# Vision tower with routed experts: when VectorE numbers the slots of the last two images

## The reference, cut to what matters

```python
probs = jax.nn.softmax(t @ Wr, axis=-1)
idx = jnp.argmax(probs, axis=-1)
onehot = jax.nn.one_hot(idx, E, dtype=jnp.int32)
pos = jnp.sum(jnp.cumsum(onehot, axis=0) * onehot, axis=-1) - 1
kept = pos < cap
flat = idx * cap + jnp.minimum(pos, cap - 1)
disp = jnp.zeros((E * cap, D), t.dtype).at[flat].add(t * kept[:, None].astype(t.dtype))
ein = disp.reshape(E, cap, D)
h = jax.nn.relu(jnp.einsum('ecd,edf->ecf', ein, W1))
eout = jnp.einsum('ecf,efd->ecd', h, W2).reshape(E * cap, D)
```

## Time and profile before

| | |
|---|---|
| time, median of 3 runs | 251.41 us (251.34 to 252.23) |
| profiled execution, its own time | 251.09 us |
| its span in the profile | 249.3 us |
| PE busy | 232.7 us (93%) |
| DVE busy | 183.8 us (74%) |
| ACT busy | 151.6 us (61%) |
| POOL busy | 98.1 us (39%) |

### The profile page before, as it was taken

How to read it: one execution, slowest core, us unless ns; L and a number is a source line. 1 busy time by engine, 2 the same in 40 slices (tenths; PEclk the granted TensorE clock), 3 DMA queues, 4 the chain that set the end, 5 groups by cost and what they waited for, 6 DMA issues and landing times.

```text
span 249.3 us, 4995 instructions
## 1 busy us (share of the span) xinstructions
PE 232.7 (93%) x1673; PEld 223.1 (89%) x1673; DVE 183.8 (74%) x557; ACT 151.6 (61%) x354; POOL 98.1 (39%) x169
## 2 busy tenths in 40 slices
PE   6999999999999999878799999999999999999940
PEld 5899999999999998647799999999999999999940
DVE  4885697887979799786456796749967678779540
ACT  5336567787877786465665477656775758656100
POOL 7000227584665658438100020156260332513662
PEclk9999999999999999999999999999999999999995
DMA  5939563174896020201499919257092460100100
GB/s 175 289 100 304 137 206 135 38 233 148 246 378 224 2 83 15 68 0 43 118 338 293 383 56 313 68 164 261 0 300 93 140 229 3 45 2 24 35 4 0
DMA packets 28378, 35.48 MB, mean 142 GB/s; under 512 B 2780, under 2 KB 25291, under 8 KB 28354
## 3 DMA queue, kind: packets, MB, share of 16 engines
q1 hardware_dynamic: 26144, 31.71, 39.9%
q0 software_dynamic: 1792, 3.47, 3.9%
q10 hardware_dynamic: 418, 0.00, 0.1%
HBM read 26.97 MB, written 9.47 MB: 146 GB/s over the span
## 4 chain that ended last, share of the span: by engine, by line
PE 75%; DMA 5%; DVE 5%; issue 5%; POOL 5%; ACT 2%; POOLq 1%; ACTq 0%; SPq 0%; DVEq 0%
PE bank L1274 14%; PE bank L1276 14%; PE bank L1275 14%; PE bank L1345 14%; PE bank L1399 4%; PE bank L1362 4%; POOL out_dram L573 3%; DMA bqc<-in_L_attn_bq_dram 2%; PE bank L1524 2%; DMA dispatched<-trow,slot 2%; PE bank L1574 2%; PE bank L1415 1%; PE bank L1373 1%; PE bank L1417 1%; PE bank L1416 1%
## 5 line engine op out<-in xcount | busy, mean ns | idle before, releaser
L1191 DVE SCALAR_TENSOR_TENSOR h_lo<-bank,h_hi 128x320 fp32r<-128x320 f32 x58 | 28.3, 488 | 27.4 <-ACT h_hi L817 24.8
L817 ACT ACTIVATE h_hi<-bank 128x320 fp32r<-128x320 f32 x58 | 25.3, 436 | 35.4 <-PE bank L1276 35.4
L573 POOL DMA_INDIRECT out_dram<-tokens_mem,images x24 | 28.0, 1168 | 37.9 <-ACT tokens_mem L834 17.1
L1274 PE MATMUL bank<-einT_hi,w_hi 128*128 128x320 f32 x128 | 40.6, 317 | 0.6 <-DVE einT_lo L1183 0.3
L1275 PE MATMUL bank<-einT_lo,w_hi 128*128 128x320 f32 x128 | 39.5, 308 | 0.0
L1276 PE MATMUL bank<-einT_hi,w_lo 128*128 128x320 f32 x128 | 39.5, 308 | 0.0
L947 DVE TENSOR_TENSOR w_lo<-w_raw,w_hi 128x1024 fp32r<-128x1024 f32 x32 | 38.8, 1214 | 0.0
L1274 PE MATMUL bank<-h_hi,w_hi 128*128 128x320 f32 x112 | 35.2, 314 | 0.1
L1276 PE MATMUL bank<-h_hi,w_lo 128*128 128x320 f32 x112 | 34.6, 309 | 0.0
L1275 PE MATMUL bank<-h_lo,w_hi 128*128 128x320 f32 x112 | 34.6, 309 | 0.0
L745 ACT ACTIVATE w_hi<-w_raw 128x1024 fp32r<-128x1024 f32 x32 | 33.7, 1052 | 0.0
(11 more groups left out here) (231 smaller groups left out, 577.3 us busy)
## 6 DMA issues: line engine op xcount, KB each, us to landing
w_raw<-in_L_ffn_W_dram SPq DMA_DIRECT2D x16, 1024.0 KB, 7.8
images<-in_x_dram SPq DMA_DIRECT2D x7, 768.0 KB, 4.8
dispatched<-blank SPq DMA_DIRECT2D x4, 645.0 KB, 8.6
images<-dispatched SPq DMA_DIRECT2D x9, 258.0 KB, 7.2
out_dram<-lone SPq DMA_DIRECT2D x8, 256.0 KB, 7.6
images<-in_x_dram SPq DMA_DIRECT2D x2, 384.0 KB, 5.1
images<-dispatched SPq DMA_DIRECT2D x9, 64.5 KB, 7.1
out_dram<-tokens_mem,images POOLq DMA_INDIRECT x24, 2.5
```

What stands on the lines that cost most here:

```text
L573: pool.indirect_dma_start(out_rows, bass.IndirectOffsetOnAxis(ap=ein[0:n, e, j, D + 1:D + 2].bitcast(U32), axis=0), z[0:n, e % 2, j, :], N ...
L817: act.activation(hidden_halves(n)[0], bank[n % 2][:, 0:CAP], ACT.Relu).then_inc(h_hi_ready, 1)
L1191: dve.scalar_tensor_tensor(lo, bank[n % 2][:, 0:CAP], 0.0, hi.bitcast(F32), ALU.max, ALU.subtract).then_inc(h_ready, 1)
L1274: pe.matmul(to, ah, bh, start=first, stop=False)
```

## The change

Four edits, all in VectorE's list:

1. In `route` the comparison with the largest gate and the product with `rank` (two instructions of 16 columns, one after the other, over tile `hit`) become one fused form for each half of the tokens (two instructions of 8 columns, with `lmax` as per-partition scalar). `lsub` moves behind `onehot`.
2. `keys_low(L)` stands ahead of `residual(L - 1)` and the two `residual_in(L, ...)`, no longer behind them.
3. `number` is cut in two: `add_places` (for images 6 and 7 `base`, and the sum `place`) and the rest. `add_places(L - 1)` stands between `softmax_sum(L)` and `late_residual()`.
4. The rest of `number(L - 1)` stands ahead of `compare(L)`, behind `factor(L - 1)`.

```diff
                 link(dve.tensor_reduce(lmax[:, :], gate[:, :, :], AX_X, ALU.max))
-                peak = lmax[:, :].unsqueeze(2).broadcast_to([P, SC, E])
-                step(dve.tensor_tensor(hit[:, :, :], gate[:, :, :], peak, ALU.is_equal))
-                if b >= 1:
-                    dve.wait_ge(lexp_ready, b)
-                dve.tensor_tensor(lsub[:, :, :], gate[:, :, :], peak, ALU.subtract).then_inc(lsub_ready, 1)
+                for s in range(SC):
+                    step(dve.scalar_tensor_tensor(hrank[:, s, :], gate[:, s, :], lmax[:, s:s + 1], rank[:, s, :],
+                                                  ALU.is_equal, ALU.mult))
                 settle()
-                link(dve.tensor_tensor(hrank[:, :, :], hit[:, :, :], rank[:, :, :], ALU.mult))
                 if b >= 2:
                     dve.wait_ge(tallied, b - 1)
                 link(dve.tensor_reduce(best[:, b % 2], hrank[:, :, :], AX_X, ALU.max))
                 dve.tensor_tensor(onehot[:, b % 2], rank[:, :, :],
                                   best[:, b % 2].unsqueeze(2).broadcast_to([P, SC, E]), ALU.is_equal
                                   ).then_inc(onehot_ready, 1)
+                if b >= 1:
+                    dve.wait_ge(lexp_ready, b)
+                dve.tensor_tensor(lsub[:, :, :], gate[:, :, :], lmax[:, :].unsqueeze(2).broadcast_to([P, SC, E]),
+                                  ALU.subtract).then_inc(lsub_ready, 1)
...
-            def number(b):
+            def add_places(b):
                 if b >= L - 1:
                     step(dve.tensor_scalar(base[:, :], best[:, b % 2], -float(CAP), float(E * CAP - 1),
                                            ALU.mult, ALU.add))
-                link(dve.tensor_reduce(place[:, :], mine[:, b % 2], AX_X, ALU.add))
-
+                step(dve.tensor_reduce(place[:, :], mine[:, b % 2], AX_X, ALU.add))
+
+            def number(b):
+                settle()
                 step(dve.tensor_scalar(over[:, :], place[:, :], float(CAP), float(NOWHERE), ALU.is_gt, ALU.mult))
...
                     compare(i - 1)
+                    add_places(i - 1)
                     number(i - 1)
...
             route(L - 1)
+            keys_low(L)
             residual(L - 1)
             residual_in(L, 0)
             residual_in(L, 1)
-            keys_low(L)
             softmax_max(L)
             moments(L - 1)
             compare(L - 1)
             softmax_sum(L)
+            add_places(L - 1)
             late_residual()
             moments(L)
             route(L)
             factor(L - 1)
+            number(L - 1)
             compare(L)
-            number(L - 1)
+            add_places(L)
             number(L)
             factor(L)
```

More of the change, by code:

```diff
@@ L176, in vit_tower_kernel @@
         lmax = sb("lmax", [P, SC])
-        hit = sb("hit", [P, SC, E])
         hrank = sb("hrank", [P, SC, E])
```

## The result

The change makes the kernel faster by 1.8 us. The median of 4 runs is 249.72 us (249.44 to 250.01), against 251.58 us (251.34 to 252.23) for 4 runs of the kernel before; the ratio is 0.9927 [0.991, 0.9945]. The prediction had 249.4, with a range from 248.9 to 250.6.

The account below looks back on a forecast made before the run. PE was taken to bound the kernel, with a 1.34 us wait for expert 1's rows at 123.46. Both paths moving earlier gain about 1.95: 251.09 - 1.95 = 249.1, plus 0.32 for the median, 249.4; range 248.9 to 250.6.

Parts of the forecast that it names:

- two clocks: PE's own work and the path slot, scatter, landing, load meet at 123.46; a gain needs both earlier.
- the rows' path: Slots of image 6, scatters, landing and SyncE's load of expert 1's rows: 1.96 us earlier.
- Low keys first: In image 7, `keys_low` ahead of the residual work makes VectorE's softmax and the steps to the gates 0.55 us earlier.
- PE's clock: PE's own work reaches the turning of expert 1's rows 0.54 us earlier, at 121.58 instead of 122.12.
- `base` and `place` in the idle place: On VectorE before image 7's residual, they fit into 0.29 us of idleness; without it they would cost 0.15 to 0.26.
- Fused comparison: In image 7's `route` on VectorE, `lmax` to `best` takes 0.59 instead of 0.65 us, a gain of 0.06.
- its cover: In other images, 0.45 us between the low keys and PE's call for them hides `route` growing by about 0.06.
- Slots of image 6: On VectorE ahead of `compare(L)`, they start at 108.80 to 108.87 and end at 109.03, 1.96 us earlier.
- The landing of the last scatter: Fourth scatter's landing, kept at 4.71 us after its start, so expert 1's rows land at 121.46 instead of 123.42.
- the picks hold the first scatter: Rival: VectorE's picks delay GpSimd's first scatter to 110.63, gain 1.15, about 250.3; 11 in 100, shared with scatters not following image 6's slots.
- the later landing: Rival: the scatters' landing takes up to 0.7 us longer, giving 249.5 to 250.1; 14 in 100.
- The slower case: Rival: longer `route` pushes `keys_low` past PE's call in images 1 to 6, giving 252.7; 4 in 100.

Follow-up runs that it names:

- a2: Kernel before with only `number` cut in two, `add_places(L - 1)` ahead of `late_residual()` and the rest ahead of `compare(L)`; 250.04 us, ratio 0.993.
- c1: a4 with the two 1024-column splits of expert weights on VectorE each cut into eight pieces of 128 columns; 250.07 us, ratio 0.9918 to the kernel before.
- b2: Changed kernel with fourteen tiny GpSimd instructions ahead of the scatters of image 7; 255.08 us in one run.
- a1: Kernel before with only `keys_low(L)` moved ahead of `residual(L - 1)` and the two `residual_in`; 251.02 us, ratio 0.9979.
- b4: Changed kernel with `base` and `place` of image 6 back in the numbering, behind `factor(L - 1)`; 249.60 us, ratio 0.9892 to the kernel before.
- a3: Kernel before with only the fused comparison in `route`, `lsub` behind `onehot`; 251.25 us, ratio 0.9991.
- a4: Changed kernel with the slots of image 6 numbered behind `compare(L)` again; 251.16 us, ratio 0.9982 to the kernel before.
- b1: Changed kernel with four tiny GpSimd instructions between the scatters of image 6 and those of image 7; 251.57 us, ratio 0.998 to the kernel before.

## Why the prediction was right, and where it was not

- **Which two clocks bound the kernel: right.** PE's own work and the rows' path met at 123.46. With the path shortened, PE goes on at its own time (after, a2, c1); with the path lengthened (b2), the wait grows.
- **Low keys first, 0.55: right.** Softmax of image 7 starts at 102.01, less 1.04 at 100.97, which is the predicted number. a1 shows 0.56 on PE's clock. The score's wait is gone.
- **`base` and `place` in the idle place, free: right.** 0.16 of it is left ahead of the residual, which is still released by PE, and b4 prices them at up to 0.30 elsewhere.
- **Fused comparison, 0.06: right in size.** `lmax` to `best` takes 109.18 - 108.57 = 0.61 instead of 0.65, where 0.59 was expected, and the pair takes 0.40 from start to the next, where the gate row gave 0.39. a3 alone moves nothing in the end. The growth of `route` in the other images stayed under its cover, as forecast: PE's busy time up to 89.10 is whole.
- **Slots of image 6 at 108.80 to 108.87, end at 109.03: right.** They start at 109.88, less 1.04 at 108.84, and end at 109.00. `mine` starts at 108.91 (108.95 expected) and the first scatter at 109.79 (109.82).
- **PE's clock at 121.58, perhaps 0.1 sooner: the gain was set 0.1 to 0.2 too small.** PE turns the rows at 121.38. PE's own shift was 0.54 in the sum; the rest of the 0.74 is the start that overlaps the end before it, 0.15 behind 122.27 with no idle time between, and the sum had up to 0.1 for that.
- **The landing of the last scatter, 4.71 kept as it was: this is the step that was mis-sized.** "The rows of expert 1 land at 121.46" rests on it, so the two clocks looked neck and neck. It measured 2.39 to SyncE's load; with the same load of some 2.5 us behind 117.57, the rows are there at about 120.1, less 1.04 at about 119.0, 2.3 us ahead of PE's need. In the traces of a1, a3, a4 and b1 the landing stays at 4.1 to 4.9, and in each of them the fourth scatter starts under a split. The prediction wrote of the long landings that they "belong to busy queues, and this place is quiet". For the loop that holds: the four scatters there that took 5.6 to 7.7 us to land had a DMA share of 0.97 to 1.05 in the 4 us from their start. But the last one had 0.11, and the two ahead of it, on queues as quiet (0.15), landed in 2.3 each in the trace of before; those rows were there to be read. It was not the queues: c1 has the same ones and lands in 2.40.
- **What it meant for the time.** Nothing for the forecast, because a shorter landing brings nothing once PE decides, which the prediction says. That the error of 2.3 us fell on the side that costs nothing was luck: no row priced the landing at its new place, and as much on the other side would have undone the gain. For the reading of the stall it means much. Had the fourth scatter of the kernel before landed in 2.39, SyncE would have loaded at 115.73 + 2.39 = 118.12 instead of 120.50, and the rows would have been in at about 121.04, ahead of PE's 122.12. By this estimate the stall of 1.34 was that one collision. No run shows it on the kernel before itself; c1 shows it on a4, whose scatters are 0.9 earlier.
- **How edits 2 and 4 add up.** Alone, a1 gives 0.85 and a2 1.47; together, with the fused pair, 2.08. Edit 4 pulls the scatters out from under the split. Edit 2 moves PE's clock, the scatters and the splits together, so by itself it leaves them beside each other.
- **The rivals.** That the picks hold the first scatter (250.3) did not come: it started 0.79 behind its slots, as predicted. Nor did the later landing; it went the other way. The slower case did not either, since `keys_low` kept its place ahead of PE's call in the steady images.
- **The median.** 249.72 is 0.3 above the forecast. From the mark to the end of PE's last matmul the trace gives a gain of 2.17 us (2.00 in the second trace of the changed kernel), the medians 1.9. Counted from the mark, the loop is left out, and there the profiled execution of before is the shortest of all twelve traces: 78.67 us from the keys of image 0 to those of image 7, where the others took 78.84 to 79.23. Of the 0.3 above the forecast, 0.17 lie in the kernel before, whose median is 251.58 beside the changed one and 251.41 in the runs that the forecast started from.

## What to carry to other kernels

When a transfer lands late, look at what runs beside the instruction that issues it before you put the delay down to the queues: here a scatter on GpSimd was held by a long subtraction on VectorE; issued ahead of it, or beside pieces of 128 columns, it landed in half the time. A duration read off one trace holds only for the neighbours that it had there, so a step that moves an instruction past an engine's long work needs that row read again. And where two clocks meet at one wait, work out the new time of each: the later of the two is the result, and what the other gains beyond that brings nothing.

## What the runs showed of the hardware

**A scatter that starts under the split is held until the split ends.** The fourth scatter, in five kernels where it meets a VectorE split of 1024 columns (fp32, two inputs in SBUF):

| kernel | scatter starts | split ends | held for | it takes | less the hold |
|---|---|---|---|---|---|
| before | 115.73 | 116.45 | 0.72 | 1.57 | 0.85 |
| a1 | 115.57 | 116.31 | 0.74 | 1.58 | 0.84 |
| a3 | 115.87 | 116.62 | 0.75 | 1.59 | 0.84 |
| a4 | 115.03 | 116.03 | 1.00 | 1.85 | 0.85 |
| b1 | 117.37 | 117.88 | 0.51 | 1.35 | 0.84 |

It always ends 0.84 or 0.85 us behind the end of the split; alone it takes 0.97. One that starts ahead of the split is not lengthened: 0.97 at 114.77 after, 0.99 at 116.07 in b1, 0.97 at 120.50 in b2. The small instructions of GpSimd are held too: `v` takes 0.19 us at 105.60 in the trace of after, 1.21 at 115.75 beside the split (115.69 to 116.91), and 0.21 in c1 between the pieces.

The Trainium skill, page "SBUF — State Buffer", says of the pair of ports that VectorE and GpSimd share that an instruction with two SBUF inputs on VectorE takes it against a GpSimd instruction that reads SBUF, for its whole length; the small instructions above agree. Its box on the DVE blocking DMA, though, names only the two-port modes, with fp32 copies as the case. Here a plain subtraction of two SBUF inputs holds an indirect DMA as well. The picks, single-source fp32, which the prediction weighed that rule on, end at 110.84 by the first scatter's start at 110.83, so they lie beside its 0.79 us of preparation and did not lengthen that. Whether they would hold the scatter itself, no run shows.

**The landing grows by more than the hold.** A free scatter is followed by SyncE's load 1.42 us behind its end (after, b2, c1). A held one needs 2.75 (a1, b1) to 3.20 us (before), so of the 2.38 by which the landing of before is longer than that of after (4.77 and 2.39), 0.60 lie in the instruction and 1.78 behind its end. In all five the load comes 2.1 to 2.5 us behind the end of the second split, which follows the first by 0.3 us. It may be that this one, which in all five starts 0.53 us ahead of the end of the scatter, holds the rest of it. A split that starts 0.05 to 0.20 us ahead of that end does no harm (after, b2, and the third scatter of before, which landed in 2.3). c1 cut both splits at once, so which of them causes that part stays open, and so does the spread from 4.1 to 4.9 among the five.
